# Four stacked graph layers on one core: order of the values, queries and keys, and the next aggregate as three fp32r products

## The chip, the core and the metric
The kernel runs on one core of one Trainium2 chip. The metric is device microseconds of one execution, the median of three timed runs. TensorE (PE) multiplies, VectorE (DVE) and ScalarE (ACT) work elementwise and empty PSUM, GpSimd (POOL) does small elementwise work, SyncE (SP) issues DMAs.

## The reference, cut to what matters
The input is 32 batches of 512 nodes with 256 features and a 512x512 adjacency for each. Four pre-normalized layers are added to x one after the other:

```
h = relu(layernorm(x));  agg = adj @ h + eps * h                     # layer 0
x = x + silu(rmsnorm(agg @ W1 + b1) * w) @ W2 + b2                   # W1: 256 x 1024
h = relu(layernorm(x));  att = sigmoid(s1_i + s2_j + c) * adj, rows normalized
x = x + att @ (h @ W.T + b)                                          # layer 1
h = relu(layernorm(x));  8 heads of 32: softmax(q k / sqrt(32) + w_h * adj, where adj) @ v
x = x + heads @ Wo.T                                                 # layer 2
h = relu(layernorm(x));  x = x + Dinv adj Dinv (h @ W3) + b3         # layer 3
```

All is float32. A product in fp32r is made of three: high by high, high by low, low by high, where the high part is the value rounded to fp32r and the low part the rest.

## The kernel before, in words
Nodes and features are tiled by 128: NT = 4 tiles of nodes, DT = 2 tiles of features. The batches are pipelined over three indices. One call of `phases(t, tf, nx)`, written out once per engine and run in a hardware loop, does layers 2 and 3 of batch t, layers 0 and 1 of batch tf = t + 1, and the aggregate of layer 0 of batch nx = t + 2. There are 30 full calls of this kind with all three, of which 29 are alike in the loop, and three partial ones. Each engine runs its own list in order and waits on semaphores for the others; there is no planner, the order is written out by hand.

A call has three parts.

The head: PE makes queries and keys of heads 0 to 3 (`project_qk(t, 0, i)`, L1310ff), then the hidden rows of the first node tile (`hidden(tf, 0, c)`), then the first half of the values (`project_v(t, 0)`). The high and low parts of q and k are made by ACT (`qk_high`, L629) and DVE (`qk_low`, L987), and DMAs restack them (`stack`, L290; the first is issued by ACT in `stack_high`).

The grid: g runs from -4 to 31. At each step PE makes one 128x512 tile of scores (`scores`, four steps ahead), DVE adds the weighted adjacency and takes the minimum (`bias`, L1001), ACT takes the exponential (`exps`, L646), PE transposes 128 columns of a head's probabilities (`turn_probs`, L1361), and ACT, or DVE for every fourth, copies them out. Between these the feed-forward of batch tf runs on: node tile n starts at step 8n - 4, and its step u = g + 4 - 8n says what is done (hidden product, Square and sum, scaling L875, tanh L587, SiLU L881, transposition L1219, high and low parts, down product in four quarters). Tile 0 has a timetable of its own (`TANH_STEPS`, `SILU_STEPS`, `LOW_STEPS`). The second half of the values stands at steps -2 and -1, q and k of heads 4 to 7 at steps 0 and 2, the degree sums of layer 3 (`degree`, L977, DVE) at 4, 6, 12 and 13.

The tail: PE does the last attention products, layer 1's attention (`attend1`, L1256), layer 3's aggregate (`aggregate3`, L1403) in two halves around `linear`, then the aggregate of batch nx in fp32 (`aggregate(nx, d)`, L1192, four 128x512 matmuls for each feature tile d), with `turn(tf)` (L1303) and `project3` between its two halves. DVE adds epsilon to the diagonal of the transposed adjacency first (`diagonal`, L854, L856) and restores it after. ACT and DVE make T_hi and T_lo (L539, L758). GpSimd computes the scales of the normalizations (L432 is the last step for a tile) and then adds b2 to the next x (`add_b2`, L440).

Memory is shared between parts: `pT`, the transposed probabilities, has several tiles of the tail over it, and `x_out`, the result of a batch, lies over `qk`. So `qk_high(t, 0, 0)` waits until the store of the batch before (L350) has landed:

```
if g == 0 and i == 0 and later(t):
    act.wait_ge(out_stored, t * 16)
```

Of the kernel before, what the change touches and what calls it, by code (L numbers as in the profile page):

```python
# [29 lines left out]
def gnn_kernel(nc, x, adj, adjT, maskT, W1, b1, rmsw, W2, b2, WL, WLn, bL, WqT, WkT, WvT, WoT, W3, b3, cols, out):  # L30
# [11 lines left out]
    with ExitStack() as ctx:  # L42
# [76 lines left out]
        msg = region[:, 5120:6144].rearrange("p (n d) -> p n d", n=NT)  # L119
        inv_x = sb("inv_x", [P, NT, HG, HD], over="hb")  # L120
# [49 lines left out]
        table_in = sem("table_in")  # L170

# [63 lines left out]
        def qk_bank(g, i):  # L235

            return (FB[2], VB)[i] if g else SB_[i]

# [143 lines left out]
        def _(pool):  # L382
# [111 lines left out]
            def phases(t, tf, nx):  # L494
# [3 lines left out]
                if t is not None:  # L498
                    degrees(t)
                    widen_inverse(t, 0)  # L500
                if tf is not None:
                    hidden_norm(tf, 2)
                    hidden_norm(tf, 3)
                    layernorm_tile(tf, 0, 1, f_norm, norm_tiles(0))
                    layernorm_tile(tf, 1, 1, f_norm, norm_tiles(0))
# [31 lines left out]
        def _(act):  # L537
# [22 lines left out]
            def norm0(tf):  # L560
                layernorm(tf, 0, f_norm, norm_tiles(0), x_new, h0)

# [76 lines left out]
            def values(t, j):  # L639
                act.wait_ge(v_ps, at(t, 2, j + 1))  # L640
                act.activation(vals[:, 2 * j:2 * j + 2, :].rearrange("p a d -> p (a d)"), VB[:, :], ACT.Copy).then_inc(v_ready, 1)
# [29 lines left out]
            def phases(t, tf, nx, prepare={}):  # L671
                b, f = t is not None, tf is not None
                if b:
                    qk_high(t, 0, 0)
                    qk_high(t, 0, 1)
                    stack_high(t)
                if f:
                    square(tf, 0, 0)
                    square(tf, 0, 1)
                if b:  # L680
                    values(t, 0)
                for g in GRID:
                    if g in prepare:
                        prepare[g]()
                    if f:
                        for n, u in tile_steps(g):
                            if n and u in (1, 2):
                                square(tf, n, u - 1)
                            elif n == 0 and u in TANH_STEPS:
                                tanh(tf, n, TANH_STEPS.index(u))  # L690
                            elif n == 0 and u in LOW_STEPS:
                                hidden_hi(tf, n, LOW_STEPS.index(u))
                            elif n and u in (4, 5):
                                tanh(tf, n, u - 4)
                            elif n and u in (6, 7):
                                hidden_hi(tf, n, u - 6)
                    if b and g == -2:
                        values(t, 1)
# [50 lines left out]
        def _(dve):  # L749
# [295 lines left out]
            def update3(t):  # L1045
                dve.wait_ge(b3_added, at(t, 1, 1))
                dve.wait_ge(dinv_ready, at(t, 1, 1))
                for n in range(NT):
# [4 lines left out]
            def phases(t, tf, nx, prepare={}):  # L1053
# [5 lines left out]
                for g in GRID:  # L1059
                    if b and g + 4 < 4 * H:  # L1060
                        bias(t, g + 4)
                    if f:
                        for n, u in tile_steps(g):
                            if u == (3 if n else 1):
                                hidden(tf, n)
                            elif n == 0 and u in SILU_STEPS:
                                silu(tf, n, SILU_STEPS.index(u))
                            elif n == 0 and u in LOW_STEPS:
                                hidden_lo(tf, n, LOW_STEPS.index(u))
                            elif n and u in (4, 5):  # L1070
                                silu(tf, n, u - 4)
                            elif n and u in (6, 7):
# [12 lines left out]
                    if b and g in DEG_STEPS:  # L1085
                        degree(t, DEG_STEPS.index(g))
                    if b and g >= 0 and g % 4 == DVE_TURN:
# [4 lines left out]
                    if b and g in QK1_LOW:  # L1092
                        qk_low(t, 1, QK1_LOW.index(g))
# [23 lines left out]
                if f:  # L1117
                    attended1(tf, 0)
                    attended1(tf, 1)
# [428 lines left out]
```

## Time and profile before

| | us |
|---|---|
| median of 3 timed runs (3564.21 to 3565.22) | 3564.24 |
| profiled execution | 3567.06 |
| its span | 3565.2 |
| mean granted clock of TensorE | 0.994 |

| engine | busy us | share of the span |
|---|---|---|
| PE | 3447.6 | 97% |
| PE weight load | 2560.3 | 72% |
| DVE | 2655.7 | 74% |
| ACT | 2286.7 | 64% |
| POOL | 943.1 | 26% |

One steady batch takes 108.7 us. Matmuls are pipelined, so busy time of PE counts the end of one and the start of the next together, and the spacing between two starts tells what one costs. An fp32 matmul is shown as two records. The 16 DMA engines are busy for 28.3% of the span in the main queue.

### The profile page before, as it was taken

The numbers are of one execution on the slowest core, as the hardware profiler recorded it, in microseconds if no ns is written. First come the engines' busy times: TensorE is split into PE (matmuls) and PEld (weight loads), VectorE is DVE, ScalarE is ACT, GpSimd is POOL, SyncE is SP. The second block draws the span as 40 slices with busy tenths as digits, with TensorE's granted clock in tenths as the row PEclk, the third lists the DMA queues.
The fourth block names the chain that finished last, engine by engine and source line by source line (L and its number), as shares of the span: only waits on it lengthen the run. The fifth ranks groups of instructions, "written<-read, shape, count | busy, mean of one in ns | idle before, by whom it ended". The sixth has DMA issues, their size and how long they took to land.

```text
span 3565.2 us, 70163 instructions
## 1 busy us (share of the span) xinstructions
PE 3447.6 (97%) x19886; PEld 2560.3 (72%) x20108; DVE 2655.7 (74%) x6794; ACT 2286.7 (64%) x5062; POOL 943.1 (26%) x2379
## 2 busy tenths in 40 slices
PE   6999999999999999999999999999999999999997
PEld 4777777777777777777777777777777777777774
DVE  6777777777787777777777877777777778777774
ACT  4666666666676666666666776666766667766664
POOL 2222331222322223322223212233222232122320
PEclk8999999999999999999999999999999999999999
DMA  3233223232232332232322223322323222323212
GB/s 102 50 94 90 76 65 88 59 95 74 73 83 64 84 94 71 65 95 53 95 77 74 79 71 77 95 71 71 89 53 95 81 75 75 76 72 95 71 54 65
DMA packets 166941, 275.09 MB, mean 77 GB/s; under 512 B 23908, under 2 KB 59876, under 8 KB 166760
## 3 DMA queue, kind: packets, MB, share of 16 engines
q1 hardware_dynamic: 164200, 269.25, 28.3%
q10 hardware_dynamic: 2560, 4.20, 0.6%
q14 instruction: 161, 1.32, 0.1%
q8 instruction: 20, 0.33, 0.0%
HBM read 122.37 MB, written 16.78 MB: 39 GB/s over the span
## 4 chain that ended last, share of the span: by engine, by line
PE 76%; issue 8%; ACT 7%; DVE 4%; DMA 3%; SPq 2%; DVEq 0%; POOL 0%; ACTq 0%; POOLq 0%
PE turn L1361 10%; PE value L1376 7%; PE score L1403 6%; PE front L1256 6%; PE front L1192 6%; PE score L1352 6%; PE front L1162 5%; PE front L1164 5%; PE front L1163 5%; ACT prob L646 3%; PE score L1349 3%; PE front L1219 2%; DMA qk_stack<-qk 2%; ACT pT L655 2%; PE score L1393 2%
## 5 line engine op out<-in xcount | busy, mean ns | idle before, releaser
L646 ACT ACTIVATE prob<-prob,small 128x512 f32<-128x512 f32 x1024 | 737.5, 720 | 351.7 <-DVE small L1001 344.3
L1001 DVE CUSTOM_DVE_ANT_0 prob<-score,adj_sb,drv 128x512 f32<-128x512 f32 x1024 | 759.2, 746 | 192.7 <-PE score L1352 184.7
L1361 PE MATMUL turn<-ident,prob 128*128 128x128 f32 x4096 | 626.1, 275 | 50.7 <-ACT prob L646 45.1
L1352 PE MATMUL score<-qk_stack 128*128 128x512 f32 x1024 | 592.2, 582 | 21.8 <-DMA qk_stack<-qk 21.7
L1361 PEld LDWEIGHTS turn<-ident,prob 128*128 128x128 f32 x4096 | 479.7, 141 | 181.4 <-issue 64.8
L655 ACT ACTIVATE pT<-turn 128x512 f32<-128x512 f32 x768 | 449.0, 585 | 72.5 <-PE turn L1361 42.3
L449 POOL TENSOR_TENSOR small<-small 128x1 f32<-128x1 f32 x128 | 24.9, 195 | 1401.2 <-ACT aside L580 1401.2
L758 DVE TENSOR_TENSOR s_lo<-front,s_hi 128x512 fp32r<-128x512 f32 x316 | 216.7, 686 | 151.5 <-ACT s_hi L539 151.5
L1349 PE MATMUL score<-unlinked,neg_mask 128*128 128x512 bf16 x802 | 306.1, 382 | 0.3 <-DVE small L1001 0.3
L1162 PE MATMUL front<-w_hi,s_hi 128*128 128x256 f32 x1024 | 300.6, 294 | 0.8 <-DVE w_lo L758 0.8
L1163 PE MATMUL front<-w_lo,s_hi 128*128 128x256 f32 x1024 | 288.3, 282 | 0.0
L1164 PE MATMUL front<-w_hi,s_lo 128*128 128x256 f32 x1024 | 287.9, 281 | 0.0
L1192 PE MATMUL front<-adjT_f,hid 128*128 128x512 f32 x512 | 234.2, 601 | 14.1 <-DVE adjT_f L856 11.7
L1376 PE MATMUL value<-pT,vals 128*32 128x512 f32 x2048 | 240.8, 599 | 0.0
L539 ACT ACTIVATE s_hi<-front 128x512 fp32r<-128x512 f32 x316 | 185.1, 586 | 86.8 <-PE front L1256 84.3
L1403 PE MATMUL score<-prob,hb 128*128 128x512 f32 x512 | 234.3, 601 | 4.5 <-ACT hb L551 4.5
L1010 DVE COPY pT<-turn 128x512 f32<-128x512 f32 x256 | 175.6, 686 | 75.2 <-PE turn L1361 75.2
L1256 PE MATMUL front<-pT,hf 128*128 128x512 f32 x512 | 227.0, 597 | 2.0 <-DVE pT L919 2.0
L875 DVE SCALAR_TENSOR_TENSOR hid<-front,small,rmsw_b 128x512 f32<-128x512 f32 x252 | 177.2, 745 | 64.0 <-POOL small L453 64.0
L881 DVE SCALAR_TENSOR_TENSOR hid<-aside,hid 128x512 f32<-128x512 f32 x256 | 176.9, 691 | 62.1 <-ACT aside L587 57.8
L1162 PEld LDWEIGHTS front<-w_hi,s_hi 128*128 128x128 f32 x1024 | 194.0, 189 | 36.4 <-issue 26.4
L1352 PEld LDWEIGHTS score<-qk_stack 128*128 128x128 f32 x1024 | 196.3, 192 | 30.6 <-DMA qk_stack<-qk 20.9
(209 smaller groups left out, 7871.6 us busy)
## 6 DMA issues: line engine op xcount, KB each, us to landing
qk_stack<-qk SPq DMA_DIRECT2D x992, 128.0 KB, 2.4
adjT_f<-in_adjT SPq DMA_DIRECT2D x32, 1024.0 KB, 5.2
adj_sb<-in_adj SPq DMA_DIRECT2D x32, 1024.0 KB, 7.5
prob<-in_adjT SPq DMA_DIRECT2D x32, 1024.0 KB, 5.3
x_new<-in_x SPq DMA_DIRECT2D x32, 512.0 KB, 4.2
out<-x_out SPq DMA_DIRECT2D x32, 512.0 KB, 3.0
qk_stack<-qk ACTq DMA_DIRECT2D x32, 128.0 KB, 2.6
pT<-in_W SPq DMA_DIRECT2D x2, 1024.0 KB, 10.9
```

Source lines behind the costliest of these rows:

```text
L646: act.activation(prob[:, i % 8, :], prob[:, i % 8, :], ACT.Exp, bias=nmax[:, h, n:n + 1], scale=-1.0, accum_out=prsum[:, h, n:n + 1]).then ...
L655: act.activation(pT[:, h % HG, j, :], TB[k % 2][:, :], ACT.Copy).then_inc(pT_act, 1)
L1001: dve.tensor_tensor_reduce(out=prob[:, i % 8, :], in0=SB_[i % 2][:, :], in1=adj_sb[:, n, :], scale=neg_w[:, h:h + 1], scalar=3e38, op0=ALU ...
L1162: pe.matmul(ps, a[0], b[0], start=start, stop=False)
L1163: pe.matmul(ps, a[0], b[1], start=False, stop=False)
L1164: return pe.matmul(ps, a[1], b[0], start=False, stop=stop)
L1192: last = pe.matmul(FB[d][:, :], h0[:, m, tile(d)], adjT_f[:, m, :], start=(m == 0), stop=(m == NT - 1))
L1256: last = pe.matmul(FB[d][:, :], hf[:, m, tile(d)], att[:, m, :], start=(m == 0), stop=(m == NT - 1))
L1352: pe.matmul(SB_[i % 2][:, :], qk_stack[:, h % 4, 0, tile(n)], qk_stack[:, h % 4, 1, :], start=False, stop=True).then_inc(sc_ps, 1)
L1361: last = pe.transpose(TB[k % 2][:, tile(n)], prob[:, (4 * h + n) % 8, tile(j)], ident[:, :])
L1376: last = pe.matmul(VB[HD * h:HD * h + HD, :], vals[:, j, P * g + HD * h:P * g + HD * h + HD], pT[:, h, j, :], start=(j == 0), stop=(j == N ...
L1403: last = pe.matmul(SB_[d][:, :], hb[:, m, tile(d)], adjT_b[:, m, :], start=(m == 0), stop=(m == NT - 1))
```

## The change
- The values: both halves are made right behind the first queries and keys, ahead of `hidden(tf, 0, c)`, the second half into a bank of its own (`v_bank(1)` is TB[0]). ACT copies both before the squares of tile 0.
- Queries and keys of heads 4 to 7: at steps -3 and -1, between the first scores; their high parts at steps 3 and 4, their low parts both at step 5.
- Node tile 0 of the feed-forward takes the timetable of the others: scaling at u = 3 (before 1), tanh and SiLU at 4 and 5, high and low parts at 6 and 7; its transposes at steps 1 and 2 (before 0 and 1).
- Degree sums at steps 13, 14, 21 and 22; GpSimd's `degrees` behind the fourth `hidden_norm`.
- The aggregate of batch nx is 24 fp32r matmuls: `aggregate_high` (8) ahead of `project3`, `aggregate_low` (16) behind `turn`, which now stands behind `project3`. ACT makes h_hi (128x1024) and af_hi (128x2048), DVE af_lo in two halves of 128x1024 and h_lo (128x1024); all four tiles lie over `pT`.
- DVE: `diagonal(nx)` moves between the two `attended1`; `update3` is cut in two, `turned(tf)` between them; T_lo of both halves is made at the head of the next call.
- ACT: `turned(tf)` stands ahead of both `aggregated`.
- The first batch's aggregate (batch 0) stays in fp32.

```diff
+        af_hi = sb("af_hi", [P, NT, N], F32R, over="pT")
+        af_lo = sb("af_lo", [P, NT, N], F32R, over="pT", skip=4 * 2048)
+        h_lo = sb("h_lo", [P, NT, D], F32R, over="pT", skip=4 * 4096)
+        h_hi = sb("h_hi", [P, NT, D], F32R, over="pT", skip=4 * 7168)
...
-        QK1_STEP, QK1_HIGH, QK1_LOW = (0, 2), (2, 4), (3, 5)
-        DEG_STEPS = (4, 6, 12, 13)
-        TANH_STEPS, SILU_STEPS, LOW_STEPS = (2, 4), (3, 4), (5, 6)
+        QK1_STEP, QK1_HIGH, QK1_LOW = (-3, -1), (3, 4), 5
+        DEG_STEPS = (13, 14, 21, 22)
...
+        def v_bank(j):
+            return TB[0] if j else VB
...
+            def rows_high(nx):
+                act.wait_ge(f_norm["ready"], at(nx, 8, 4))
+                hi(h_hi[:, :, :], h0).then_inc(h_hi_ready, 1)
+            def adjacency_high(nx):
+                act.wait_ge(diag_eps, at(nx, 1, 1))
+                act.wait_ge(att_added, at(nx, 3, 0))
+                hi(af_hi[:, :, :], adjT_f[:, :, :]).then_inc(af_hi_ready, 1)
...
                     stack_high(t)
+                    values(t, 0)
+                    values(t, 1)
                 if f:
                     square(tf, 0, 0)
                     square(tf, 0, 1)
-                if b:
-                    values(t, 0)
...
                 if nx is not None:
                     norm0(nx)
+                    rows_high(nx)
                 if b:
                     gathered(t, 0)
+                if nx is not None:
+                    adjacency_high(nx)
+                if b:
                     gathered(t, 1)
                 if f:
                     layernorm(tf, 0, b_norm, norm_tiles(50), x2, hf)
+                    turned(tf)
                 if nx is not None:
                     aggregated(nx, 0)
-                if f:
-                    turned(tf)
-                if nx is not None:
                     aggregated(nx, 1)
...
+            def rows_low(nx):
+                dve.wait_ge(h_hi_ready, at(nx, 1, 0))
+                lo(h_lo[:, :, :], h0, h_hi[:, :, :]).then_inc(h_lo_ready, 1)
+            def adjacency_low(nx):
+                dve.wait_ge(b_norm["normed"], at(nx, 5, -1))
+                dve.wait_ge(af_hi_ready, at(nx, 1, 0))
+                for m in (slice(0, 2), slice(2, 4)):
+                    lo(af_lo[:, m, :], adjT_f[:, m, :], af_hi[:, m, :]).then_inc(af_lo_ready, 1)
...
                 if f:
                     attended1(tf, 0)
-                    attended1(tf, 1)
-                    factors1(tf)
                 if nx is not None:
                     diagonal(nx)
                 if f:
+                    attended1(tf, 1)
+                    factors1(tf)
                     update1(tf)
                 if b:
                     gathered(t, 0)
                     gathered(t, 1)
                 if nx is not None:
-                    aggregated(nx, 0)
+                    adjacency_low(nx)
+                    rows_low(nx)
+                if b:
+                    update3(t, (0,))
                 if f:
                     turned(tf)
                 if b:
-                    update3(t)
+                    update3(t, (1, 2, 3))
 
             def next_aggregate(nx):
+                aggregated(nx, 0)
                 aggregated(nx, 1)
                 restore_diagonal(nx)
...
+            def aggregate_high(nx):
+                pe.wait_ge(h_hi_ready, at(nx, 1, 0))
+                pe.wait_ge(af_hi_ready, at(nx, 1, 0))
+                pe.wait_ge(msg_ready, at(nx, 4, 0))
+                for d in range(DT):
+                    for m in range(NT):
+                        pe.matmul(FB[d][:, :], h_hi[:, m, tile(d)], af_hi[:, m, :], start=(m == 0), stop=False)
+            def aggregate_low(nx):
+                for m in range(NT):
+                    if m % 2 == 0:
+                        pe.wait_ge(af_lo_ready, at(nx, 2, m // 2 - 1))
+                    for d in range(DT):
+                        pe.matmul(FB[d][:, :], h_hi[:, m, tile(d)], af_lo[:, m, :], start=False, stop=False)
+                pe.wait_ge(h_lo_ready, at(nx, 1, 0))
+                for d in range(DT):
+                    for m in range(NT):
+                        last = pe.matmul(FB[d][:, :], h_lo[:, m, tile(d)], af_hi[:, m, :], start=False, stop=(m == NT - 1))
+                    last.then_inc(agg_ps, 1)
...
                     project_qk(t, 0, 0)
                     project_qk(t, 0, 1)
+                if b:
+                    project_v(t, 0)
+                    project_v(t, 1)
                 if f:
                     hidden(tf, 0, 0)
                     hidden(tf, 0, 1)
-                if b:
-                    project_v(t, 0)
...
                 if nx is not None:
-                    aggregate(nx, 0)
+                    aggregate_high(nx)
...
+                if b:
+                    project3(t, tf)
                 if f:
                     turn(tf)
-                if b:
-                    project3(t, tf)
                 if nx is not None:
-                    aggregate(nx, 1)
+                    aggregate_low(nx)
```

## Rows read from the trace of the kernel before

**Rows 1.** The page, busy time of each engine: us, share of span, instructions.
```profile
PE 3447.6 (97%) x19886; PEld 2560.3 (72%) x20108; DVE 2655.7 (74%) x6794; ACT 2286.7 (64%) x5062; POOL 943.1 (26%) x2379
```

**Rows 2.** Windows of one batch: stretch, length, busy us of each engine (instructions), clock, DMA.
```profile
1071.49:1081.57 10.08, 10.08 (x49) 6.44 (x48) 5.03 (x12) 4.25 (x8) 4.54 (x11) 1.00 0.10 36
1081.57:1089.99 8.42, 7.94 (x40) 6.47 (x39) 3.60 (x5) 3.71 (x8) 0.88 (x3) 1.00 0.42 97
1089.99:1095.72 5.73, 5.15 (x28) 3.82 (x28) 5.03 (x12) 4.26 (x12) 0.06 (x1) 1.00 0.94 206
1095.72:1103.20 7.48, 7.48 (x45) 6.39 (x47) 6.45 (x16) 6.72 (x16) 0.00 (x0) 1.00 0.18 38
1103.20:1110.57 7.37, 6.78 (x44) 5.84 (x43) 5.51 (x12) 5.70 (x16) 0.94 (x3) 1.00 0.35 75
1110.57:1180.20 69.63, 69.45 (x423) 50.72 (x428) 56.75 (x158) 46.51 (x102) 22.96 (x58) 1.00 0.26 75
```

**Rows 3.** Timeline, PE, tail and head: start, us, engine, line, operation, count.
```profile
1071.49 3.60 PE L1192 MATMUL front<-adjT_f,hid 128*128 128x512 f32 x8
1074.93 1.04 PE L1303 MATMUL turn<-ident,hf 128*128 128x128 f32 x8
...
1082.20 0.39 PE L1163 MATMUL score<-bT_lo,wp_hi 128*128 128x512 f32 x1
1082.43 0.39 PE L1164 MATMUL score<-bT_hi,wp_lo 128*128 128x512 f32 x1
...
1087.99 0.28 PE L1162 MATMUL value<-wp_hi,bT_hi 128*128 128x256 f32 x1
1088.10 0.28 PE L1163 MATMUL value<-wp_lo,bT_hi 128*128 128x256 f32 x1
```

**Rows 4.** Groups by form in the set-up (0 to 80 us): busy us, mean ns.
```profile
L539 ACT ACTIVATE w_hi<-pT 128x2048 fp32r<-128x2048 f32 x2 | 3.8, 1906 | 3.8 <-DMA rmsw_b<-in_rmsw 3.8
...
L758 DVE TENSOR_TENSOR w_lo<-pT,w_hi 128x2048 fp32r<-128x2048 f32 x2 | 4.6, 2288 | 0.0
L758 DVE TENSOR_TENSOR wp_lo<-wp_raw,wp_hi 128x1536 fp32r<-128x1536 f32 x1 | 1.8, 1757 | 0.0
```

**Rows 5.** Timeline of all engines, same batch, from the tail to the first score.
```profile
1071.68 1.34 DVE L758 TENSOR_TENSOR a_lo<-score,a_hi 128x512 fp32r<-128x512 f32 x2
...
1073.40 2.78 POOL L440 TENSOR_TENSOR x_in<-x_new,b_b 128x256 f32<-128x256 f32 x4
...
1079.61 0.40 SPq L350 DMA_DIRECT2D out<-x_out  x1
...
1083.63 0.69 ACT L629 ACTIVATE qk<-score,drv 128x512 fp32r<-128x512 f32 x1 [0.86 <-PE score L1164]
...
1084.92 0.60 ACT L629 ACTIVATE qk<-score 128x512 fp32r<-128x512 f32 x1 [0.60 <-PE score L1164]
...
1089.99 0.49 PE L1352 MATMUL score<-qk_stack 128*128 128x512 f32 x1 [0.48 <-DMA qk_stack<-qk]
```

**Rows 6.** Lines L903 and L919, all batches: duration ns min/median/max.
```profile
L903 DVE CUSTOM_DVE_ANT_0 hid<-hf,wa x128: 392/420/644, 70.2 to 3440.8; 128x256 f32<-128x256 f32 x128
...
L919 DVE SCALAR_TENSOR_TENSOR pT<-pT,mask_sb,adjT_f x128: 737/748/1747, 76.6 to 3446.9; 128x512 f32<-128x512 f32 x128
```

**Rows 7.** Timeline of the last batch's head.
```profile
3472.13 0.39 SPq L350 DMA_DIRECT2D out<-x_out  x1
...
3475.17 0.69 ACT L629 ACTIVATE qk<-score,drv 128x512 fp32r<-128x512 f32 x1 [7.01 <-DMA out<-x_out]
```

**Rows 8.** Timeline, ACT, the stages of node tile 0.
```profile
1096.12 0.72 ACT L646 ACTIVATE prob<-prob,small 128x512 f32<-128x512 f32 x1
...
1096.84 0.58 ACT L655 ACTIVATE pT<-turn 128x512 f32<-128x512 f32 x1
1097.32 0.59 ACT L539 ACTIVATE s_hi<-front 128x512 fp32r<-128x512 f32 x1
...
1108.34 0.72 ACT L646 ACTIVATE prob<-prob,small 128x512 f32<-128x512 f32 x1 [1.67 <-DVE small L1001]
```

More of the change, by code:

```diff
@@ L170, in gnn_kernel @@
         table_in = sem("table_in")
+        h_hi_ready, h_lo_ready, af_hi_ready, af_lo_ready = (
+            sem(n) for n in ("h_hi_ready", "h_lo_ready", "af_hi_ready", "af_lo_ready"))
         unlinked_ready, deg_ready = sem("unlinked_ready"), sem("deg_ready")
@@ L503, in phases @@
                     hidden_norm(tf, 3)
+                if t is not None:
+                    degrees(t)
+                if tf is not None:
                     layernorm_tile(tf, 0, 1, f_norm, norm_tiles(0))
@@ L640, in values @@
                 act.wait_ge(v_ps, at(t, 2, j + 1))
-                act.activation(vals[:, 2 * j:2 * j + 2, :].rearrange("p a d -> p (a d)"), VB[:, :], ACT.Copy).then_inc(v_ready, 1)
+                act.activation(vals[:, 2 * j:2 * j + 2, :].rearrange("p a d -> p (a d)"), v_bank(j)[:, :], ACT.Copy).then_inc(v_ready, 1)
             def exps(t, i):
@@ L688, in phases @@
                                 square(tf, n, u - 1)
[L689 to L693, printed above, removed]
+                            elif u in (4, 5):
                                 tanh(tf, n, u - 4)
-                            elif n and u in (6, 7):
+                            elif u in (6, 7):
                                 hidden_hi(tf, n, u - 6)
-                    if b and g == -2:
-                        values(t, 1)
                     if b and g in QK1_HIGH:
@@ L1043, in gathered, with update3 @@
                 lo(a3_lo[:, d, :], SB_[d][:, :], a3_hi[:, d, :]).then_inc(agg3_lo, 1)
[L1045 to L1048, printed above, removed]
+            def update3(t, which):
+                if which[0] == 0:
+                    dve.wait_ge(b3_added, at(t, 1, 1))
+                    dve.wait_ge(dinv_ready, at(t, 1, 1))
+                for n in which:
                     dve.wait_ge(proj3_ps, at(t, 4, n + 1))
@@ L1063, in phases @@
                         for n, u in tile_steps(g):
-                            if u == (3 if n else 1):
+                            if u == 3:
                                 hidden(tf, n)
[L1066 to L1070, printed above, removed]
+                            elif u in (4, 5):
                                 silu(tf, n, u - 4)
-                            elif n and u in (6, 7):
+                            elif u in (6, 7):
                                 hidden_lo(tf, n, u - 6)
@@ L1086, in phases @@
                         degree(t, DEG_STEPS.index(g))
+                    if b and g == QK1_LOW:
+                        qk_low(t, 1, 0)
+                        qk_low(t, 1, 1)
                     if b and g >= 0 and g % 4 == DVE_TURN:
@@ L1325, in project_qk, with project_v @@
                 last.then_inc(qk_ps, 1)
-            def project_v(t, j, parts=(0, 1)):
-                if j and 0 in parts:
-                    pe.wait_ge(v_ready, at(t, 2, 1))
-                elif not j and later(t):
+            def project_v(t, j):
+                if not j and later(t):
                     pe.wait_ge(o_ready, at(t, 3, 0))
-                for i in parts:
+                for i in range(2):
                     for k in range(DT):
                         s = tile(2 * j + i)
-                        last = product(VB[:, D * i:D * i + D], (bT_hi[:, k, s], bT_lo[:, k, s]),
+                        last = product(v_bank(j)[:, D * i:D * i + D], (bT_hi[:, k, s], bT_lo[:, k, s]),
                                        (wp_hi[:, WV, k, :], wp_lo[:, WV, k, :]), k == 0, k == DT - 1)
-                if 1 in parts:
-                    last.then_inc(v_ps, 1)
+                last.then_inc(v_ps, 1)
             def scores(t, i):
@@ L1359, in turn_probs @@
                 wait_bank(t, k)
+                if h == 0 and v_bank(1) is TB[k % 2]:
+                    pe.wait_ge(v_ready, at(t, 2, 2))
                 for n in range(NT):
@@ L1457, in phases @@
                                 down(tf, n, q)
-                    if b and g in (-2, -1):
-                        project_v(t, 1, (g + 2,))
                     if b and g < 0:
                         scores(t, g + 4)
+                    if b and g in QK1_STEP:
+                        project_qk(t, 1, QK1_STEP.index(g))
                     if b and g >= 0:
                         turn_probs(t, g // 4, g % 4)
-                    if b and f and g in (0, 1):
-                        turn_hidden(tf, 0, g)
+                    if b and f and g in (1, 2):
+                        turn_hidden(tf, 0, g - 1)
                     if b and g == 4 * HG + 3:
```

9 lines of the change are left out of this document (1 added, 8 removed).

## The prediction, made before the result was known
> **What bounds the kernel.** I read the page's busy table first: PE is busy 97% of the span [rows 1]. A busy share of pipelined matmuls is an average, so next I cut one steady batch (108.7 us, 29 of them alike) into windows [rows 2]. PE has no gap in the tail window (10.08 of 10.08) or in the long stretch of scores and feed-forward (69.45 of 69.63). It has gaps in three short windows at the head of the batch: 8.42 - 7.94 = 0.48, 5.73 - 5.15 = 0.58 and 7.37 - 6.78 = 0.59 us. So a batch is PE's work plus about 1.7 us of waiting, all at the head. Reading the timeline at those three places names the waits: the first score waits for a DMA, the other two for exponentials, the last of which wait for DVE; their rows stand further down. The granted clock is 1.00 (2.4 GHz) in every window, so clock plays no part.
>
> The profiled run took 3567.06 us (span 3565.2), the median of the timed runs is 3564.24. I make the sum against 3567.1 and take off 2.8.
>
> **1. The aggregate as three fp32r products (PE).** Before, it is 2 x 4 fp32 matmuls, shown as 2 x 8 records. The first half starts at 1071.49 and what follows it at 1074.93: 3.44 us, 0.43 a record; both halves 6.87 us. The fp32r projections behind the second start 0.23 apart (1082.20, 1082.43), and fp32r products of half the columns 0.11 (1087.99, 1088.10) [rows 3]. The change issues 24 of 512 columns: 24 x 0.231 = 5.54 us. PE saves 1.33 us a batch if no operand is late. The price is bounded by the half-width 0.11 (24 x 0.11 = 2.6, a saving of 4.3) and by the fp32 record's 0.43 (10.3, a loss of 3.4); I take 0.231, whose width and type are the same.
>
> **2. What the halves cost ACT and DVE.** ACT adds one Identity of 128x1024 and one of 128x2048. The latter took 1.91 us in the set-up [rows 4]; the former lies between a 512-column 0.6 and that, by the slope 1.04. They stand behind norm0 (end 1065.3) and around gathered(0), so af_hi is there at about 1068.9, and PE wants it at 1071.5, when aggregate3(1) ends. The second gathered comes only then too. Hidden, with 2.6 us to spare. The diagonal moves ahead of attended1(1) on DVE, which there waits for ACT; its load has landed by then. Nothing gained or lost; were the load late, linear would be too, 1 us for 1 us.
>
> DVE adds three subtractions of 128x1024. 2048 columns took 2.29 us and 1536 took 1.76 [rows 4], so 1.2 each, spaced 1.15. They stand behind gathered(1) (end 1073.0, [rows 5]) and behind the last of the second normalization's tiles, which GpSimd finishes just after 1073.4, where its next work starts. Behind them on DVE: update3(0), the low halves of the turned rows, update3(1 to 3). Waiting for those: PE's next projection, and the store of x_out, which the next batch's qk_high waits for, since x_out lies over qk.
>
> PE's new order, from 1071.5: aggregate_high 1.85 (to 1073.35), project3 2.75 (1076.1), turn 0.9 (1077.0), aggregate_low 3.7 (1080.7). Were DVE alone on the memory, the halves are there at 1074.7 and 1075.8, and h_lo, wanted at 1078.9, at 1077.0.
>
> But GpSimd's add_b2, four additions of SBUF operands, starts at 1073.40 [rows 5], 0.1 us before DVE may begin. Where a DVE instruction with two SBUF operands meets a GpSimd addition, one waits for the other: L903 takes 0.420 us as a rule and 0.644 beside GpSimd, L919 0.748 and 1.747 [rows 6]. In the second case DVE came 0.07 us behind a GpSimd addition of 1.27 us and ended 0.55 after it, 0.2 less than its own length. So I alternate them, with 0.2 of overlap: DVE's three run 1073.95-1075.2, 1075.6-1076.8, 1077.2-1078.4. PE still gets each in time (wanted 1077.0, 1077.9, 1078.9). The tail is late by 0.5 to 1.2 us where it isn't PE's: update3(0) 1078.4, low halves of the rows to 1080.0, update3(1 to 3) to 1081.2.
>
> The Trainium skill (SBUF — State Buffer, "SBUF: two separate sides") says this outright: VectorE with two SBUF inputs and a GpSimd instruction that reads SBUF take a shared port pair as an exclusive lock, and the loser fully blocks. By that rule the three subtractions cost up to 3 x 0.7 us more, without it nothing; the rows of L919 and L903 agree with it.
>
> **3. The store becomes the last to arrive.** Before, it is issued at 1079.61, 0.2 behind DVE's last update, lands 3.0 later (1082.65), and qk_high starts at 1083.63, behind PE. In the last batch the store is late and qk_high starts exactly at its landing: 3472.13 + 3.04 = 3475.17 [rows 7]. In the changed kernel: 1081.2 + 0.25 + 3.0 = 1084.45, where PE (projection from 1080.7) would allow 1082.4. The second qk_high follows 0.6 later, at 1085.1. From its start to the first score are 1089.99 - 1084.92 = 5.07 us (stacking DMAs, [rows 5]). First score: 1090.15, against 1089.99 before. PE could have started it at 1080.7 + 2.8 (projections) + 2.7 (both values) + 3.3 (hidden) = 1089.5. So of 1.33 saved none is left here; without the lock the first score comes at 1089.5, -0.5.
>
> **4. Values and second projections moved, first tile's steps later.** PE's work is the same. Both values come ahead of the first score, so the 0.5 us of DMA wait is covered. Between the first scores stand only the projections. First turn of probabilities: 5.4 behind the first score instead of 5.73 (it waits for the fourth exponential, which no longer stands behind values). Then the price: hidden, tanh, SiLU of tile 0 run two steps later, where PE has little of its own. ACT does four exponentials, two tanh, two high halves, three copies and one qk_high there; exponential and copy start 0.72 and 0.48 apart (1096.12, 1096.84, 1097.32) [rows 8], the others about 0.55, some 7.1 us in all, and the tanh-SiLU pair on one buffer adds waits of about 1. I get 8.15 us for the stage that took 7.48; bounds are 6.1 (PE's own work there, its 7.48 without the 1.4 of a projection that has moved away) and 9 (two more of those waits). In the next stage the degrees are gone from DVE, whose queue made the ACT wait of 1.67 us [rows 8]; PE's gap of 0.59 goes: 6.78. Sum -0.33 + 0.67 - 0.59 = -0.25. Degrees at steps 21 and 22 stand ahead of hidden(3): between 0 and 0.4, I take 0.1. On GpSimd degrees move behind hidden_norm(3); it is idle there.
>
> **Sum.** A steady batch: +0.15 (first score) - 0.25 + 0.1 = 0.0, say -0.05; 30 batches -2, and about -1.5 in the last batch alone, whose second values now fill a DMA wait. 3567.1 - 3.5 = 3563.6; less 2.8: **3561 us**. A difference under 0.2% (7 us) can't be told from none.
>
> **The rivals.**
> A: forecast, the store late through DVE and GpSimd in turns. For it: [rows 5 to 7]. Against it: the alternation is seen on short instructions only. 3561, own range 3549 to 3573.
> B: DVE isn't held up beyond the first addition, or the store lands by 1083.5. Then the first score is PE's: -0.5 - 0.25 + 0.1 = -0.65 a batch, x 30 = -19.5, with the last batch and the 2.8 off 3543. Own range 3534 to 3551. For it: a DVE queue without gaps may keep GpSimd out.
> C: the head costs nothing, as PE's queue runs ahead there: B with the 8.15 at 7.2, -1.6 a batch: 3515. Against it: ACT's list is 7.1 us long without any wait.
> D, slower: the lock holds DVE through all four additions (to 1076.2). The halves come at 1077.3, 1078.5 and 1079.6; PE stalls 1 us in aggregate_low, the store lands at 1085.7, first score 1091.3, +1.3 a batch less 0.15: +1.1, 3600. It decides from 0.25 us a batch: as soon as the store lands after 1084.8. Half of it (the stage of tile 0 at 9) gives 3580.
>
> **How the numbers follow.** A 0.42, B 0.28, C 0.08, D 0.22 (0.12 in full, 0.10 its half). A is centred near no change and 24 us wide, so I split it 0.13 faster, 0.21 same, 0.08 slower; B and C are faster, D slower. Faster 0.49, same 0.21, slower 0.30. The range takes A, B and the half of D, and leaves out C and the full D, 0.2 together: 3534 to 3584.
>
> **What would show it.** Right: 24 matmuls of aggregate, 0.23 apart, none waiting; the three new subtractions stretched as L919 is (mean over 1.5 us instead of 1.2); ACT's qk_high released by the DMA of x_out in nearly every batch; a PE gap of 1 to 2 us between first and second head's turns; no gap before step 8. Wrong: subtractions at 1.2 us, qk_high released by PE (then B), PE waiting for af_lo or h_lo (then D).

## The result and the profile after

The changed kernel takes 3588.91 us (median of 4 runs, 3586.66 to 3590.70), the kernel before, beside it, 3564.73 (4 runs, 3564.21 to 3567.38): ratio 1.0066, 95% interval 1.0049 to 1.0083. That is 24 us slower, where I forecast 3 us faster, and 5 us above my range. The profiled run took 3587.84 us, its span is 3586.0.

The page of the changed kernel, busy time of each engine, and its chain of waits:
```profile
PE 3453.6 (96%) x20356; PEld 2593.0 (72%) x20356; DVE 2807.8 (78%) x6887; ACT 2367.1 (66%) x5124; POOL 1049.2 (29%) x2379
...
PE 49%; DVE 18%; issue 10%; ACT 8%; POOL 7%; DMA 5%; SPq 2%; ACTq 0%; POOLq 0%; DVEq 0%
```
PE is busy about as long as in [rows 1], in a longer span. The chain now goes through DVE, POOL and DMA for 30% of its length (7% in the kernel before, where POOL has none of it): there are waits between engines in every batch. The windows of the same steady batch (columns as in [rows 2]), from the first matmul of the aggregate, with the same six events as limits:
```profile
1078.48:1088.07 9.59, 9.59 (x59) 8.29 (x58) 9.11 (x15) 4.25 (x8) 7.86 (x13) 1.00 0.00 1
1088.07:1097.65 9.58, 9.15 (x53) 7.55 (x51) 4.78 (x8) 4.18 (x9) 0.00 (x0) 1.00 0.48 123
1097.65:1103.03 5.38, 5.13 (x21) 3.27 (x22) 3.80 (x10) 3.16 (x10) 0.93 (x3) 1.00 0.94 210
1103.03:1111.14 8.11, 6.91 (x39) 5.02 (x40) 6.91 (x16) 6.66 (x16) 0.00 (x0) 1.00 0.19 41
1111.14:1117.89 6.75, 6.75 (x44) 5.89 (x44) 5.33 (x12) 6.03 (x17) 0.93 (x3) 1.00 0.44 96
1117.89:1187.83 69.94, 69.51 (x427) 50.64 (x427) 57.28 (x159) 49.45 (x104) 23.02 (x56) 1.00 0.26 74
```
Against [rows 2], window by window: -0.49, +1.16, -0.35, +0.63, -0.62, +0.31. The limit of the first window moved by itself: the first fp32r matmul behind an fp32 one is recorded 0.4 us earlier than an fp32 one would be. So I count from attend1 from here on, which is the same work on both sides, and take medians over 22 batches of each trace. Turn n is the first transposition of probabilities (`turn_probs`) for the n-th score tile, counted from 0. The kernels of the experiments stand in the same table; they are told of below.

```
us, medians   attend1 to   to first  turns   turns   turn 8 to     period
              first score  turn      0 to 4  4 to 8  next attend1
before          36.02       5.73     7.48    7.35      52.16       108.73
changed         36.24       5.38     8.12    6.74      52.90       109.38
e1              36.25       5.38     8.12    6.82      52.15       108.70
e2              36.24       5.38     8.12    6.74      52.12       108.59
e3              36.24       5.73     7.48    7.35      52.15       108.95
e4              36.75       5.46     8.12    6.74      52.90       109.97
e5              35.86       5.38     8.12    6.74      52.92       109.01
e6              35.52       5.46     8.12    6.74      52.90       108.75
e7              35.80       5.39     8.12    6.82      52.15       108.27
e8              36.04       5.73     7.48    7.35      52.15       108.75
e9              34.76       5.72     7.48    7.34      52.22       107.52
e10             35.54       5.46     8.12    6.82      52.21       108.16
e11             36.04       5.72     7.48    7.34      52.21       108.77
e12             35.98       5.73     7.48    7.34      52.15       108.70
```
The row of e8 is over all 31 batches. In e5, e7 and e8 the first score moves from batch to batch between about 35.8 and 36.45 (of the 29 inner batches of e8, 13 lie under 35.95 and 15 at 36.2 or more), so a median over part of the batches can come out 0.3 too long; the means over the 29 inner batches are 36.02, 35.94 and 36.09.

The period grew by 0.65 us, and 31 times that is 20.2 of the 20.8 us between the spans. By stage: +0.22 - 0.35 + 0.64 - 0.61 + 0.74.

The tail of the changed kernel, timeline of the same batch, against [rows 5]:
```profile
1080.80 5.78 POOL L449 TENSOR_TENSOR x_in<-x_new,b_b 128x256 f32<-128x256 f32 x4
1080.85 3.45 DVE L775 TENSOR_TENSOR af_lo<-adjT_f,af_hi 128x1024 fp32r<-128x1024 f32 x2 [0.44 <-POOL small L441]
...
1084.22 1.76 DVE L775 TENSOR_TENSOR h_lo<-hid,h_hi 128x1024 fp32r<-128x1024 f32 x1
...
1088.27 0.47 DVE L1080 SCALAR_TENSOR_TENSOR x_out<-front,small,x_out 128x256 f32<-128x256 f32 x1
...
1088.97 0.40 SPq L359 DMA_DIRECT2D out<-x_out  x1
...
1090.81 0.28 PE L1193 MATMUL value<-wp_hi,bT_hi 128*128 128x256 f32 x1
...
1091.97 0.69 ACT L650 ACTIVATE qk<-score,drv 128x512 fp32r<-128x512 f32 x1 [3.10 <-DMA out<-x_out]
...
1097.65 0.50 PE L1402 MATMUL score<-qk_stack 128*128 128x512 f32 x1 [0.43 <-DMA qk_stack<-qk]
```
The four additions of POOL take 5.78 us instead of 2.78, DVE's first two subtractions 3.45, and ACT's qk_high waits for the store, in 31 batches (waits of ACT: total us, times, longest):
```profile
ACT qk L650 <- DMA out<-x_out: 99.0, 31, 5.2
```

### The profile page after: what moved, and what is told of

Same layout as the page of the kernel before. It is cut to its first block, busy times and chain, and to the rows that moved or that the text cites. A ratio compares the mean times of both kernels' runs of the same rounds, so it can differ in the third digit from the quotient of the medians.

```text
span 3586.0 us, 71217 instructions
## 1 busy us (share of the span) xinstructions
PE 3453.6 (96%) x20356; PEld 2593.0 (72%) x20356; DVE 2807.8 (78%) x6887; ACT 2367.1 (66%) x5124; POOL 1049.2 (29%) x2379
## 4 chain that ended last, share of the span: by engine, by line
PE 49%; DVE 18%; issue 10%; ACT 8%; POOL 7%; DMA 5%; SPq 2%; ACTq 0%; POOLq 0%; DVEq 0%
PE turn L1413 11%; PE value L1428 6%; PE score L1402 5%; PE front L1193 5%; PE front L1195 5%; PE front L1194 5%; PE score L1399 5%; DVE pT L948 3%; DMA out<-x_out 3%; DVE af_lo L775 3%; DMA qk_stack<-qk 2%; PE front L1272 2%; ACT prob L667 2%; DVE prob L1030 2%; POOL small L439 2%
## 5 line engine op out<-in xcount | busy, mean ns | idle before, releaser
L1399 PE MATMUL score<-unlinked,neg_mask 128*128 128x512 bf16 x1024 | 391.0, 382 | 1.8 <-DVE unlinked L1001 1.7
L481 POOL TENSOR_TENSOR inv_x<-small,drv 128x128 f32<-128x128 f32 x256 | 100.4, 424 | 677.1 <-DVE small L1046 677.1
L910 DVE SCALAR_TENSOR_TENSOR hid<-aside,hid 128x512 f32<-128x512 f32 x256 | 176.7, 690 | 77.0 <-ACT aside L608 76.8
L1194 PEld LDWEIGHTS front<-w_lo,s_hi 128*128 128x128 f32 x1024 | 193.3, 189 | 15.3
```

What stands on the lines that cost most here:

```text
L1194: pe.matmul(ps, a[0], b[1], start=False, stop=False)
L1399: pe.matmul(SB_[i % 2][:, :], neg_mask[:, h, :], unlinked[:, n, :], start=True, stop=False)
```

## The experiments

### e1 and e2: the degree sums
e1 puts the sums where they were (and GpSimd's use of them, behind its second hidden_norm):
```
-        DEG_STEPS = (13, 14, 21, 22)
+        DEG_STEPS = (4, 6, 12, 13)
```


> The changed kernel with the four degree sums back at steps 4, 6, 12 and 13 on VectorE, and GpSimd's use of them back behind its second hidden_norm; all else as changed. Theory T (the mis-sized term of my sum: the degree sums at 13, 14, 21 and 22 delay the hidden layer of tiles 2 and 3, 0.7 us a batch instead of 0.1): from the ninth turn of probabilities to the first matmul of attend1 52.89 falls to 52.2 us; the stage before it (steps 4 to 8), 6.74 now, gets its old wait back and rises to between 6.9 and 7.35. Together between 0 and -0.5 us a batch, 3573 to 3589. Rival H (what is late there is set by the new order of the first tile and of the values, not by the degree sums): 52.9 stays, and only the stage before gets longer: 3595 to 3607.

e2 shortens them, so that the degrees are left out of the computation:
```
-                dve.tensor_reduce(deg[:, n:n + 1], adj_sb[:, n, :], AX.X, ALU.add)
+                dve.tensor_reduce(deg[:, n:n + 1], adj_sb[:, n, 0:8], AX.X, ALU.add)
```


> The changed kernel whose degree sums read 8 of 512 columns at the same steps (the degrees are left out of the computation in that way); same instructions and waits. Theory T: with 0.68 us of VectorE become some 0.1, four times, the ninth turn to attend1 falls from 52.89 to 52.2 us or a little below, the rest of the batch stays: -0.7 us a batch, 3566 (3562 to 3570). Rival H: 52.9 within 0.1, 3586 to 3590.

Measured: e1 3567.13 us, 1.0002 of before (0.9993 to 1.0011), better than either theory's time; e2 3563.38, 0.9992 (0.9983 to 1.0001). In both the long stretch is back at 52.15 and 52.12: all of its +0.74 hangs on the degree sums. The old places cost less here than I expected, 0.08 in turns 4 to 8. Split by turns, the sums at 13 and 14 make turns 12 to 20 go from 18.69 to 19.10, those at 21 and 22 make turns 20 to 28 go from 13.89 to 14.25. In e1 two sums stand at 12 and 13, and turns 12 to 20 take no longer than in e2 (18.69 and 18.68): it is the step from 12 and 13 to 13 and 14 that costs. The waits in the changed kernel, then in e1 (total us, times, longest):
```profile
PE turn L1413 <- ACT prob L667: 45.3, 100, 2.0
PEld front L1272 <- DVE hid L910: 47.9, 96, 3.5
```
```profile
PE turn L1411 <- ACT prob L665: 36.3, 69, 2.0
PEld front L1270 <- DVE hid L908: 40.7, 65, 3.9
```
31 more of each, one in every batch. They lie in different places. In turns 12 to 20 PE's weight load waits 0.24 us a batch for `hid`, DVE's SiLU product (L910); in turns 20 to 28 PE waits 0.28 us a batch for an exponential. That is 0.52 of the 0.74; the rest isn't recorded as a wait.

### e3 and e4: each half of the change alone
e3 is the kernel before with what the change does to the aggregate (its new halves, update3 split, rows turned behind the projection); e4 is the kernel before with the rest (values, second queries and keys, tile 0, degree sums). Both are made of the change's own lines:
```
e3:  QK1_STEP, QK1_HIGH, QK1_LOW = (0, 2), (2, 4), (3, 5)     e4:  aggregate(nx, 0)
     DEG_STEPS = (4, 6, 12, 13)                                    turn(tf)
     aggregate_high(nx)                                            project3(t, tf)
     project3(t, tf)                                               aggregate(nx, 1)
     turn(tf)                                                      QK1_STEP, QK1_HIGH, QK1_LOW = (-3, -1), (3, 4), 5
     aggregate_low(nx)                                             DEG_STEPS = (13, 14, 21, 22)
```


> The kernel before with only the aggregate changed (three fp32r products, the new halves on ScalarE and VectorE, update3 split, rows turned behind the projection); values, second queries and keys, tile 0 and degrees as before. Theory T (the aggregate saves 1.33 us on TensorE and the late store takes all of it back, first score 0.1 to 0.2 later; the head as it was): period 108.7 + 0.15 = 108.85, 3564 to 3572. Rival L (the halves and the locked port cost more than that, also without the new head): over 3575. Rival B (without the new head the store isn't late, the saving of 0.5 shows): 3545 to 3555.

> The kernel before with only the head and the degree sums changed (values ahead of the scores, second queries and keys between scores, tile 0 two steps later, degrees at 13, 14, 21, 22); aggregate in fp32 as before. Theory T: first turn -0.35 behind the first score, next stage +0.68, next -0.61, ninth turn to attend1 +0.7, so +0.4 us a batch, and the first score later by up to 0.3 if both values now stand on the path of the store or the projection: 3577 to 3587. Rival L (the loss needs the new aggregate): 3555 to 3568.

Measured: e3 3577.91 us, 1.0035 (1.0023 to 1.0048). The time is 6 us above Theory T's range and in that of Rival L, but the stages are T's: only the first score is later, by 0.22, which makes 7 us of the 10.8 between the spans. The other 4 are the clock. In e3 PE stands idle for 1.65 to 2.35 us in front of the first score of every steady batch (about 0.5 in the kernel before, 0.4 in the changed one), and in four of these batches the granted clock is 0.50 (1.2 GHz) for 3.4 us from 0.3 to 1.3 us behind that score; the period of those four is 110.0 us instead of 108.95. The gap in these four was 2.01 to 2.04 us; six other batches had gaps as long and kept the clock at 1.00. The windows around one of the four (columns as in [rows 2]):
```profile
982.50:985.90 3.40, 1.36 (x8) 1.08 (x9) 0.57 (x1) 0.67 (x2) 0.93 (x3) 1.00 0.93 196
985.90:989.30 3.40, 3.40 (x14) 2.94 (x13) 2.85 (x8) 2.60 (x7) 0.00 (x0) 0.50 0.91 207
```
e4 3607.03, 1.0114 (1.0099 to 1.0130), slower than any theory: its first score is 0.73 later, because the second half of the values (12 products, 0.115 apart, 1.4 us) now stands on PE ahead of it, and the DMA wait that could cover it was 0.5 us in a steady batch of the kernel before (21.7 us in 32 waits, 5.1 of them in the last batch). That leaves 0.9, of which 0.15 stays unexplained. In e4 PE has no gap there: the first score is PE's own. The two losses don't add up: in the changed kernel PE's longer list, shorter by the aggregate's saving, lies beside the late store, and the later of the two counts.

### e5 and e6: the lock and the store
e5 lets GpSimd's add_b2 wait:
```
                     pool.wait_ge(x1_ready, at(tf, 4, 0))
+                    pool.wait_ge(h_lo_ready, at(tf, 1, 0))
```


> The changed kernel with one wait added on GpSimd: add_b2 starts only when VectorE has written h_lo, so that VectorE's three new subtractions have the shared memory to themselves. Theory S (the subtractions and GpSimd's additions take turns; that makes the last update and so the store of x_out late, and the store sets the first score): the three take 1.15 to 1.2 us instead of 1.76, the store lands 1.5 us earlier, qk_high is released by TensorE, the first score comes 0.6 to 0.8 us earlier behind attend1 (36.24 to 35.5, where TensorE's own list ends by the kernel with only the head changed: 36.75 less 1.33), the rest of the batch stays: -0.7 a batch, 3567 (3563 to 3572). Rival G (the additions, now later, hold up VectorE's low halves and updates just as long): subtractions 1.2, store no earlier, 3585 to 3592. Rival N (turns are not the cause): subtractions stay above 1.6.

e6 moves x_out:
```
-        x_out = sb("x_out", [P, NT, D], over="qk")
+        x_out = sb("x_out", [P, NT, D], over="prob", skip=4 * 2048)
...
-                if g == 0 and i == 0 and later(t):
-                    act.wait_ge(out_stored, t * 16)          (ScalarE, qk_high)
+                if i == 4 and later(t):
+                    dve.wait_ge(out_stored, t * 16)          (VectorE, bias)
```


> The changed kernel with x_out laid over two of the eight tiles of prob that are free in the tail, instead of over qk; ScalarE's first qk_high no longer waits for the store, VectorE's fifth bias does. Theory S: the store is off the path although the subtractions still take 1.76; the first score is TensorE's own, 35.4 to 35.6 behind attend1 instead of 36.24: -0.75 a batch, 3565 (3561 to 3570). Rival V (VectorE's low halves of the rows, also late, then hold the projection): -0.3 or less, over 3577.

Durations (ns, min/median/max) in the changed kernel, then in e5:
```profile
L775 DVE TENSOR_TENSOR af_lo<-adjT_f,af_hi x62: 1722/1764/1776, 96.6 to 3379.5; 128x1024 fp32r<-128x1024 f32 x62
L775 DVE TENSOR_TENSOR h_lo<-hid,h_hi x31: 1752/1757/1761, 99.9 to 3381.2; 128x1024 fp32r<-128x1024 f32 x31
L449 POOL TENSOR_TENSOR x_in<-x_new,b_b x128: 722/1717/1728, 24.3 to 3381.8; 128x256 f32<-128x256 f32 x128
```
```profile
L776 DVE TENSOR_TENSOR af_lo<-adjT_f,af_hi x62: 1216/1223/1228, 95.3 to 3369.4; 128x1024 fp32r<-128x1024 f32 x62
L450 POOL TENSOR_TENSOR x_in<-x_new,b_b x128: 721/737/753, 23.4 to 3373.9; 128x256 f32<-128x256 f32 x128
```
The turns at the shared memory are shown: 1.76 us becomes 1.22, 1.72 becomes 0.74. e6 takes 3569.28 us, 1.0009 (1.0000 to 1.0018), in its range, with the first score at 35.52: the store was what set it. e5 takes 3580.11, 1.0039 (1.0026 to 1.0053), between the ranges of Theory S and Rival G and a gain of less than half of what I expected: the first score only came to 35.86. Its timeline shows why:
```profile
1082.02 0.40 SPq L359 DMA_DIRECT2D out<-x_out  x1
1082.80 0.69 DVE L776 TENSOR_TENSOR T_lo<-front,T_hi 128x512 fp32r<-128x512 f32 x1 [1.01 <-ACT T_hi L551]
1085.79 0.69 ACT L651 ACTIVATE qk<-score,drv 128x512 fp32r<-128x512 f32 x1 [2.73 <-DMA out<-x_out]
1085.84 0.69 DVE L776 TENSOR_TENSOR T_lo<-front,T_hi 128x512 fp32r<-128x512 f32 x1 [2.35 <-issue]
```
The store is issued 1.1 us earlier, but lands 3.7 us behind its issue instead of 3.0; and DVE stands 2.35 us in front of its second T_lo, waiting for nothing that the profile shows.

### e7 and e8: both edits, with the degree sums back, and with the old head


> Both of these edits, and the degree sums back at steps 4, 6, 12 and 13. By Theory S and the result for the degree sums (0.68 a batch): 3567.1 - 31 x 0.8 = 3542 (3536 to 3548), faster than both kernels. If the two edits' gains were to add up rather than be the same gain: 3520.

> Both of these edits on the kernel with only the aggregate changed, values, second queries and keys, tile 0 and degree sums as in the kernel before. There TensorE's list ahead of the first score is shorter by the second projection of queries and one value, so the stacking DMAs behind qk_high set it: 36.02 less the 1.33 of the aggregate = 34.7 behind attend1, against 36.24 now. 3577.9 - 31 x 1.5 = 3531 (3525 to 3540): the head's change then is a loss of 0.3 a batch. Rival: another wait appears at the first exponentials, and no more than half is left, 3550 to 3560.

Measured: e7 3554.47 us, 0.9968 (0.9956 to 0.9980), faster than both kernels but 6 us above its range; e8 3564.72, 0.9997 (0.9988 to 1.0006), 13 us less than e3 where I expected 47, and above its rival's range too. The timeline of e8, DVE:
```profile
1078.09 0.47 DVE L1081 SCALAR_TENSOR_TENSOR x_out<-front,small,x_out 128x256 f32<-128x256 f32 x1
1079.81 0.69 DVE L774 TENSOR_TENSOR T_lo<-front,T_hi 128x512 fp32r<-128x512 f32 x1 [1.25 <-ACT T_hi L546]
1083.26 0.69 DVE L774 TENSOR_TENSOR T_lo<-front,T_hi 128x512 fp32r<-128x512 f32 x1 [2.76 <-issue]
1083.86 0.42 DVE L893 COPY adjT_f<-aside 128x512 f32<-128x512 f32 x1
1084.20 0.74 DVE L1015 SCALAR_TENSOR_TENSOR qk<-score,drv,qk 128x512 fp32r<-128x512 f32 x1
```
Both T_lo stand at the top of DVE's loop over the batches. Its compare-and-branch is issued 24.3 us behind attend1 (at 1076.7), the first T_lo behind it starts about 3.0 us later, and then a second gap follows.

### e9 to e12: DVE's loop jump
e9 is e8 with DVE's loop written out, e10 is e7 with the same, e11 the kernel before:
```
-            with dve.Fori(1, B - 2) as t:
+            for t in range(1, B - 2):
```


> The kernel of e8 (aggregate changed, add_b2 late, store aside, head as before) with VectorE's loop over the batches written out straight, so that VectorE has no jump. Seen in e8: VectorE's compare-and-branch is issued 24.3 us behind attend1, the first instruction behind it comes at 27.2, the next only at 30.7, and the second low half of T (its operand there at 27.5) at 30.8; the low halves of queries and keys, the stacking DMAs and the first score follow. Theory J (the instructions behind the jump come late): without it the second T_lo is at 27.9 to 28.0, the low halves follow ScalarE's high ones (28.9), first score 34.7 instead of 36.3, -1.5 a batch: 3564.7 - 46 = 3519 (3512 to 3528). Rival K (VectorE waits there for something else that the profile doesn't name): T_lo stays at 30.8, 3562 to 3568.

> The kernel of e7 (changed head, degree sums back, add_b2 late, store aside) with VectorE's loop written out straight. Theory J: second T_lo from 30.2 to 27.9, first score from 35.80 to TensorE's own 35.5: -0.3 a batch, 3554.5 - 9 = 3546 (3541 to 3550); less than in e9, because both values stand on TensorE ahead of the first score here. Rival K: 3552 to 3557.

> The kernel before with VectorE's loop written out straight, a control. Theory J: there the jump ends before its operand comes (T_hi at 28.75, T_lo at 28.8), so nothing hangs on it: 3562 to 3568. If straight code by itself were a gain or a loss elsewhere in the batch, it would show here.

e12 is e8 with the store held back:
```
                     sp.wait_ge(out_ready, at(t, 4, 4))
+                    if nx is not None:
+                        sp.wait_ge(T_lo_ready, at(nx, 2, 2))
```


> The kernel of e8 with the store of x_out issued only when VectorE's second T_lo is written. VectorE's second instruction behind the jump came 2.2 us behind the first in the changed kernel (store issued at 27.5), 3.4 in e8 (store issued at 26.3). Theory Q (the store's packets delay the loading of VectorE's code): with no store in flight it comes 1.2 to 2.2 behind, T_lo before 29.6, and the first score at 35.3 to 36.0 unless the store then delays the stacking DMAs. Rival R (the gap is the jump's own): T_lo at 30.7 still; 3562 to 3590, as the store then meets the stacking.

Measured: e9 3527.30 us, 0.9897 (0.9882 to 0.9912); e10 3550.18, 0.9955 (0.9942 to 0.9969); e11 3568.36, 1.0009 (1.0000 to 1.0018); e12 3561.04, 0.9987 (0.9978 to 0.9996). e9's time is in its range, e10's and e11's are less than 0.5 us above theirs. The first scores of e9 and e10, 34.76 and 35.54, are those of Theory J, which is borne out; e12's second T_lo, at 29.6, and first score, at 35.98, are those of Theory Q. DVE in e9:
```profile
1067.50 0.47 DVE L1081 SCALAR_TENSOR_TENSOR x_out<-front,small,x_out 128x256 f32<-128x256 f32 x1
1068.39 0.69 DVE L774 TENSOR_TENSOR T_lo<-front,T_hi 128x512 fp32r<-128x512 f32 x1 [0.42 <-ACT T_hi L546]
1069.30 0.69 DVE L774 TENSOR_TENSOR T_lo<-front,T_hi 128x512 fp32r<-128x512 f32 x1 [0.21 <-ACT T_hi L546]
1069.90 0.42 DVE L893 COPY adjT_f<-aside 128x512 f32<-128x512 f32 x1
1070.76 0.75 DVE L1015 SCALAR_TENSOR_TENSOR qk<-score,drv,qk 128x512 fp32r<-128x512 f32 x1 [0.44 <-ACT qk L643]
```
What DVE's T_lo waited for (total us, times, longest), in the changed kernel, e8 and e12; the kernel before and e9 have no such row, there all is waiting for ACT (last row, the kernel before):
```profile
DVE T_lo L775 <- issue: 44.8, 28, 1.8
```
```profile
DVE T_lo L774 <- issue: 72.3, 28, 2.9
```
```profile
DVE T_lo L777 <- issue: 46.1, 28, 1.8
```
```profile
DVE T_lo L758 <- ACT T_hi L539: 193.3, 63, 4.8
```
28 times is once per pass back through the loop. The page's row of the instruction queue (packets, MB, share), in e8 and in e9:
```profile
q14 instruction: 161, 1.32, 0.1%
```
```profile
q14 instruction: 79, 0.65, 0.1%
```
82 packets fewer for 28 jumps less, three for each jump. The trace has the start of each packet (8 KB): behind every jump there are three. In e8 they start 25.3, 28.9 and 31.2 us behind attend1 (medians), with the jump at 24.3, the first T_lo at 27.3 and the second at 30.6; in e12 at 25.3, 27.7 and 30.2, with the second T_lo at 29.6; in e9 there is none at this place. So code that is loaded by DMA after a jump fits both gaps. e12 shows that the store lengthens the second: with no store in flight the stall per jump is 1.6 us instead of 2.6 (46.1 and 72.3 over 28). It is a store already under way that does it: in the changed kernel, which issues the store at 27.5, 0.2 us before the second packet, that packet starts at 27.7 and the stall is 1.6 as well; in e8 the store is issued at 26.4. e12 itself gains little, as its store then meets the stacking DMA that ACT issues (3.5 us to landing instead of 2.5). The store is slower in e8 too; its landing, median from issue, in the changed kernel and in e8:
```profile
out<-x_out SPq DMA_DIRECT2D x32, 512.0 KB, 3.0
```
```profile
out<-x_out SPq DMA_DIRECT2D x32, 512.0 KB, 3.7
```
In e9, with the store issued at the same 26.4 and no jump, it is 3.0. Two packets fall into the flight of the changed kernel's store and don't slow it, so what slows the one in e8 isn't known beyond its having to do with the jump.

The Trainium skill (Runtime: NRT & Kernel Launch, "Instruction fetch mechanics") says that a taken branch whose target isn't in the two pages of code at hand forces a DMA fetch before execution goes on. The packets and the stall agree with it; how many instructions a page has, no run here shows.

e9 is faster than both kernels, by 38 us (1.0%) than the one before. In it DVE's code is written out 29 times. The changed kernel itself was not run with DVE's loop written out.

## Why the prediction was wrong, point by point

1. **The step that failed: the last item of step 4, "Degrees at steps 21 and 22 stand ahead of hidden(3): between 0 and 0.4, I take 0.1".** The four sums cost 0.74 us a batch (e1, e2). Over 31 batches this is 23 us of the 24 between the two kernels, and, less the 0.1 that I had, 20 us of the 28 between forecast and result; without them (e2, 3563.38) the result would have been inside the range. Those at 21 and 22 cost 0.36, near the upper end of my bound of 0.4, where I took 0.1. Those at 13 and 14 cost 0.41, and I gave them no price: two sums stood at 12 and 13 before, and the move by one step went in as nothing, without a reason. In that window ([rows 2], last row) PE had almost no gap, so a late operand shows in the time at once. 0.68 us of DVE at 14 instead of 12 delays the SiLU product whose transposition PE does next, and at 21 and 22 instead of 4 and 6 it delays a bias, and with it the exponential that PE takes next. A low share of DVE in a window (56.75 of 69.63 there) is room only where no one waits for the next DVE instruction.
2. **Aggregate, -1.33 (step 1): right.** attend1 to the end of the first projection of queries and keys, the last product counted by its pitch of 0.23: 30.70 us in the median batch of e4, 29.39 in e6, -1.31.
3. **The lock (step 2, rival A): right.** DVE and POOL take turns, instruction by instruction: one pair comes every 1.69 us (3.45 for two, less 1.76 for the second), where 1.22 and 0.74 alone make 1.96. Rival B's free DVE and rival D's DVE held through four additions are both refuted. D's prices were also off by its own terms: its 3600 leaves out the 2.8 us that the other sums take off, and a stage of tile 0 at 9 instead of 8.15 gives 3587, outside the stated range, not 3580. The stage took 8.12, so that the result lies near 3587 has another cause. The Trainium skill's rule (SBUF — State Buffer, "SBUF: two separate sides"), that the loser fully blocks for the whole of the other's instruction, is borne out up to that overlap of 0.27 us.
4. **The store as the last to arrive (step 3): right.** qk_high waits for it in 31 batches; first score +0.22 where I had +0.15. I put PE's own time at 18.0 us behind the start of the old aggregate, 35.5 behind attend1; e6 has 35.52.
5. **The head (step 4): right.** -0.35, +0.64, -0.61 against -0.33, +0.67, -0.59. That the values cost nothing ahead of the first score holds only beside the shorter aggregate and the late store: in e4 the first score is 0.73 later.
6. **What I missed without its deciding here.** DVE's jump. In the kernel before, its stall ends before T_hi is there (193 us of T_lo's waits are for ACT), and e11 shows that it costs nothing. In the changed kernel it is 1.6 us long and lies beside the late store: the second T_lo starts 29.6 us behind attend1, qk_high at 30.5. A faster version meets it: e5 makes rival B's condition true, a DVE that isn't held up, and has the first score at 35.86, not at the 35.5 that B's 3543 needs. I had no rival for that. Nor had I one for the clock: in e3, where PE's gap ahead of the first score is about 2 us, it fell in four batches.

That leaves the forecast's -0.05 a batch against +0.65: +0.64 from the degree sums (0.74 less the 0.1 that I had), +0.07 from the first score, -0.07 from the head, and 0.05 that I had rounded. These 0.70 a batch are 22 of the 28 us. The last batch came out 0.4 us shorter where I had 1.5, and the first attend1 0.6 later. The timed medians lie 24.2 us apart and the spans 20.8; these 3.4 us are unexplained, and the interval of the ratio (17 to 30 us) covers them.

## What to carry to other kernels

Price every instruction that is moved, on an engine that isn't the bound too, by who waits for the next instruction behind its new place, not by that engine's share of the window; moving it by one step is a move. When one wait is taken off a path, look up what each other engine does at that moment before giving the gain a number, the jump of its loop among it: a row "issue" in front of the first instructions of a loop body is time for which the profile has no name. Put the jump where nobody waits for that engine and no large transfer is in flight (not tried here beyond holding the store back, e12), or write the loop out (e9, e10).

## What the runs showed of the hardware that was not expected

- DVE's jump back in its loop: 2.8 us or more until the first instruction (a register operation), 5.2 to 6.6 until the second T_lo (changed kernel, e5 to e8, e12), three packets of the instruction queue each; ACT's compare-and-branch, in a steady batch of e6, is followed by its next instruction 0.26 us later (26.93 and 27.19 behind attend1). Why the one engine stalls and the other not, no run tells.
- A store of 512 KB issued 2.1 us behind the jump (e8) lengthens the second stall from 1.6 to 2.6 us (e12, no store in flight) and itself lands after 3.7 us instead of 3.0 (e9, no jump).
- The granted clock fell to 0.50 for 3.4 us in four steady batches of e3, each time behind a gap of 2.0 us of PE, and cost 1.0 us each time; behind six other gaps as long it stayed at 1.00. In the steady batches of the kernel before and of the changed one, with gaps of about 0.5 us, and in those of e12, with 1.3 to 1.6 us, it never fell.
- Behind an fp32 group the first fp32r matmul is followed by the second only 0.63 us later (in the kernel before at 1081.57, where [rows 2] have their limit, and 1082.20, [rows 3]), where 0.23 is the pitch. So a saving by a change of type is counted between points that have the same types around them: 1.31 us here, and 0.49 in the first window above.
